# Block moves of an attention kernel: two destination buffers, two issuing queues, fewer tiles moved

## The reference

```python
h = _layernorm(x) * (1 + ca) + sa
x = x + ga * attention(h, w_qkv, w_out)      # 16 heads of 64, causal, softmax over 2048 keys
h = _layernorm(x) * (1 + cb) + sb
x = x + gb * ffn(h, ...)                     # one of 8 experts for each token, 128 -> 512 -> 128, relu
```

## Time and profile before

| | us |
|---|---|
| median of 2 runs (1029.2 to 1029.48) | 1029.34 |
| the profiled execution | 1032.4 |
| its span, first to last instruction | 1030.6 |
| PE busy / VectorE busy / ScalarE busy / GpSimd busy | 919.4 / 758.8 / 626.7 / 110.2 |

### The profile page before, as it was taken

One profiled execution on the slowest core, in us unless ns is written; L12 is line 12 of the kernel. 1 busy time (PEld: TensorE's weight loads), 2 busy tenths in 40 slices (PEclk: granted clock), 3 DMA queues, 4 the chain that ended last, 5 costly groups with the idle time before them and its releaser, 6 DMA issues.

```text
span 1030.6 us, 18821 instructions
## 1 busy us (share of the span) xinstructions
PE 919.4 (89%) x6147; PEld 681.8 (66%) x6147; DVE 758.8 (74%) x2400; ACT 626.7 (61%) x1159; POOL 110.2 (11%) x125
## 2 busy tenths in 40 slices
PE   3999989898998989998989899998999899868797
PEld 2676657675676757675767667675766566546697
DVE  4898748794797848894879578875898389774454
ACT  2876548574685648665757468564875466542375
POOL 0200001000100010000200010001000011101244
PEclk9999989999999999999999999999999899988899
DMA  3005430353014520543036302551053201356020
GB/s 77 11 22 132 106 72 14 90 135 84 21 48 112 120 50 12 127 110 84 14 73 148 87 21 53 127 113 36 23 118 87 66 6 46 95 155 174 25 64 26
DMA packets 154306, 76.91 MB, mean 75 GB/s; under 512 B 20647, under 2 KB 151507, under 8 KB 154210
## 3 DMA queue, kind: packets, MB, share of 16 engines
q1 hardware_dynamic: 152962, 73.58, 29.7%
q0 software_dynamic: 1248, 2.13, 0.7%
HBM read 18.21 MB, written 11.77 MB: 29 GB/s over the span
## 4 chain that ended last, share of the span: by engine, by line
PE 38%; SPq 27%; DVE 17%; DMA 8%; issue 6%; ACT 3%; another core or an unknown queue 1%; POOLq 0%; POOL 0%; DVEq 0%; ACTq 0%
SPq L667 24%; PE ps L910 11%; DMA turned_far<-staged 7%; PE ps L874 6%; PE ps L885 6%; DVE staged L1269 6%; PE ps L853 4%; DVE probs L1254 4%; PE ps L857 3%; PE ps L1034 2%; PE ps L1045 2%; DVE probs L1257 2%; SPq L686 1%; SPq L697 1%; ACT probs L1099 1%
## 5 line engine op out<-in xcount | busy, mean ns | idle before, releaser
L1099 ACT ACTIVATE probs<-probs,neg_max 128x128 f32<-128x128 f32 (+15 forms) x256 | 308.9, 1207 | 150.2 <-DVE neg_max L1261 147.3
L874 PE MATMUL ps<-k_both,q_both 128*128 128x512 f32 (+2 forms) x1280 | 358.8, 397 | 9.0 <-DVE probs L1254 2.8
L1254 DVE TENSOR_SCALAR_CACHE_REDUCE probs<-ps 128x512 f32<-128x512 f32 (+1 forms) x384 | 245.5, 666 | 22.5 <-PE ps L885 10.8
L874 PEld LDWEIGHTS ps<-k_both,q_both 128*128 128x128 f32 x1280 | 203.7, 189 | 78.7 <-issue 28.7
L1107 ACT COPY pT<-ps 128x512 f32<-128x512 f32 (+1 forms) x342 | 178.1, 549 | 113.5 <-PE ps L885 104.8
L885 PE MATMUL ps<-ident,probs 128*128 128x128 f32 x1472 | 213.1, 274 | 1.4 <-ACT probs L1099 0.5
L885 PEld LDWEIGHTS ps<-ident,probs 128*128 128x128 f32 x1472 | 174.8, 141 | 42.3 <-issue 15.4
L910 PE MATMUL ps<-pT,v_sb 128*64 128x256 f32 (+1 forms) x1600 | 174.3, 366 | 9.9 <-DVE oT L1305 7.5
L910 PE MATMUL ps<-turned_far,v_sb 128*64 128x256 f32 x704 | 104.1, 454 | 58.7 <-DMA turned_far<-staged 58.7
L910 PEld LDWEIGHTS ps<-pT,v_sb 128*64 128x64 f32 x1600 | 108.2, 137 | 72.8 <-issue 12.4
L1257 DVE CUSTOM_DVE_ANT_0 probs<-ps,causal 128x256 f32<-128x256 f32 (+3 forms) x256 | 130.6, 510 | 26.4 <-PE ps L874 26.1
(11 more groups left out here) (145 smaller groups left out, 680.5 us busy)
## 6 DMA issues: line engine op xcount, KB each, us to landing
turned_far<-staged SPq DMA_DIRECT2D x384, 96.0 KB
x_sorted<-blank SPq DMA_DIRECT2D x19, 458.5 KB, 5.2
rinv_b<-spread_rows SPq DMA_DIRECT2D x128, 64.0 KB, 2.7
turned_far<-staged SPq DMA_DIRECT2D x128, 64.0 KB
spread_rows<-rinv_rows SPq DMA_DIRECT2D x256, 0.5 KB
probs<-in_L_ffn_W_dram SPq DMA_DIRECT2D x1, 2048.0 KB, 9.5
w_pair<-in_L_attn_w_qkv_dram SPq DMA_DIRECT2D x24, 64.0 KB, 2.1
hT<-x_sorted SPq DMA_DIRECT2D x23, 65.5 KB
```

The source lines that it names most:

```text
L874: m = pe.matmul(ps_ring[:, s.bank, 0:w], q_split[r % 2][:, q0:q0 + P], k_split[r % 2][:, part, k0:k0 + w], start=(part == 0), stop=(part = ...
L1099: act.activation(row, row, ACT.Exp, bias=neg_max[:, g, r:r + 1], accum_out=row_sum[:, g, r:r + 1]).then_inc(exp_done, 1)
L1254: dve.tensor_scalar(row, ps_ring[:, bank, 0:w], 1.0, LOWEST, ALU.mult, ALU.max, accum_out=highest).then_inc(bank_free[bank], 1)
```

## The change

`turned_far` gets two buffers (`FAR_BUFS`), so a move waits for the far value matmuls of the move before the last; `staged` keeps one. SP issues the steps a = 0 and 1 of each move and GpSimd the steps a = 2 and 3, in a list with the K doublings that is sorted by the planner's times. Each destination buffer and each queue has a semaphore of its own, and PE and VectorE wait for both queues' halves. Groups 5, 6 and 7 have 5 far tiles instead of 6, so that 53 of a pair's 72 tiles are near. `pT` has 5 slots instead of 8, and the planner's constants change. The small tables of the last stage lie in `staged` instead of `pT`.

```diff
-PT_SLOTS = 8
-STAGED = 6
-FAR = {4: 4, 5: 6, 6: 6, 7: 6}
-ISSUE = 430.0
+PT_SLOTS = 5
+STAGED = 5
+FAR = {4: 4, 5: 5, 6: 5, 7: 5}
+FAR_BUFS = 2
+ISSUE = 650.0
 LAND = 4000.0
-PV_BATCH = 8
+PV_BATCH = 4
 SCORE_LEAD = 1.4
-SCORE_TILES = 18.0
-TAKE_ACT = 0.0
-TAKE_DVE = 2500.0
-ADD_DVE = 0.0
-PROJ_LEAD = 2
+SCORE_TILES = 16.0
+TAKE_ACT = -800.0
+TAKE_DVE = 600.0
+ADD_DVE = 1000.0
+PROJ_LEAD = 2.5
...
+        steps = [(self.at("lo", p, c, 1), "double", (p, c)) for p, c in parts]
+        for m, (p, g) in enumerate(self.moves):
+            steps += [(self.move_at(m)[0] + 4 * ISSUE * i, "move", (p, g, 2 + i)) for i in range(2)]
+        self.pool = [Step(kind, key, 0, 0) for _, kind, key in sorted(steps)]
...
             begin = max(self.at("shuffle", p, g, r) for r in range(4))
+            if m >= FAR_BUFS:
+                q, f = self.moves[m - FAR_BUFS]
+                begin = max(begin, self.at("pv", q, f, far(f) - 1))
             if m:
-                q, f = self.moves[m - 1]
-                begin = max(begin, self.at("pv", q, f, far(f) - 1), self.move_at(m - 1)[0] + 16 * ISSUE)
+                begin = max(begin, self.move_at(m - 1)[0] + 8 * ISSUE)
...
-            self.moved[m] = begin + HOP, begin + HOP + 16 * ISSUE + LAND
+            self.moved[m] = begin + HOP, begin + HOP + 8 * ISSUE + LAND
...
-            for a in range(4):
+            for a in range(2):
                 steps.append((self.move_at(m)[0] + 4 * ISSUE * a, "move", (p, g, a)))
...
-        turned_far = sb("turned_far", [P, STAGED, P // SQUARE, 4 * SQUARE])
+        turned_far = sb("turned_far", [P, FAR_BUFS, STAGED, P // SQUARE, 4 * SQUARE])
...
+        def move_blocks(queue, key, landed):
+
+            p, g, a = key
+            m = plan.move_no[p, g]
+            queue.wait_ge(shuffled, 4 * m + 4)
+            if m >= FAR_BUFS:
+                q, f = plan.moves[m - FAR_BUFS]
+                queue.wait_ge(pv_done, plan.order[q, f, far(f) - 1] + 1)
+            for b in range(P // SQUARE):
+                queue.dma_start(turned_far[b * SQUARE:(b + 1) * SQUARE, m % FAR_BUFS, 0:far(g), a, :],
+                                staged[a * SQUARE:(a + 1) * SQUARE, 0:far(g), b, :]).then_inc(landed[m % 2], 16)
...
-            for p in range(PAIRS):
-                for c in range(NC):
+            for s in plan.pool:
+                if s.kind == "move":
+                    move_blocks(pool, s.key, moved_soft)
+                    continue
...
-                            pe.wait_ge(moved, 256 * plan.move_no[p, g] + 256)
+                            for landed in (moved, moved_soft):
+                                pe.wait_ge(landed[plan.move_no[p, g] % 2], 128 * (plan.move_no[p, g] // 2) + 128)
...
                     if m and r == 0:
-                        dve.wait_ge(moved, 256 * m)
+                        for landed in (moved, moved_soft):
+                            dve.wait_ge(landed[(m - 1) % 2], 128 * ((m - 1) // 2) + 128)
```

More of the change, by code:

```diff
@@ L508, in adaln_block @@
         blank = sb("blank", [P, ROW])
-        turned_all = pT[:].rearrange("p s c -> p (s c)")
-        hidT = turned_all[:, 0:4 * FF].rearrange("p (s f n) -> p s f n", s=4, f=FT)
-        table_end = [4 * FF]
+        hidT = pT[:, 0:4, :].rearrange("p s (f n) -> p s f n", f=FT)
+        staged_all = staged[:].rearrange("p j b c -> p (j b c)")
+        table_end = [0]
         def table(n, width):
@@ L517, in table @@
             table_end[0] = first + n * width
-            return turned_all[:, first:first + n * width].rearrange("p (r c) -> p r c", c=width)
+            return staged_all[:, first:first + n * width].rearrange("p (r c) -> p r c", c=width)
         PAD_E = NE // 2
@@ L585, in adaln_block @@
         shuffled = sem("shuffled")
-        moved = sem("moved")
+        moved = [sem(f"moved{i}") for i in range(2)]
+        moved_soft = [sem(f"moved_soft{i}") for i in range(2)]
         pv_done = sem("pv_done")
@@ L658, in _ @@
                 if s.kind == "move":
[L659 to L668, removed]
+                    move_blocks(sp, s.key, moved)
                 elif s.kind == "w1":
@@ L716, in _ @@
                                  blank[:].unsqueeze(1).broadcast_to([P, end - first, ROW])).then_inc(blanked, 16)
-            sp.wait_ge(moved, 256 * len(plan.moves))
+            for i in range(2):
+                sp.wait_ge(moved[i], 128 * len(range(i, len(plan.moves), 2)))
+                sp.wait_ge(moved_soft[i], 128 * len(range(i, len(plan.moves), 2)))
             sp.wait_ge(chosen_known, 1)
@@ L763, in _ @@
             pool.wait_ge(numbered, 1)
-            for p in range(PAIRS):
-                for c in range(NC):
[L767 to L779, removed]
+            for s in plan.pool:
+                if s.kind == "move":
+                    move_blocks(pool, s.key, moved_soft)
+                    continue
+                p, c = s.key
+                k_bank, k_use = plan.bank_of("proj", p, c, 1)
+                pool.wait_ge(bank_free[k_bank], k_use + 1)
+                cols = slice(c * BANK, (c + 1) * BANK)
+                for h in range(2):
+                    if h:
+                        pool.wait_ge(k_doubled[c], 2 * p + 1)
+                    elif c:
+                        pool.wait_ge(k_doubled[c - 1], 2 * p + 2)
+                    elif p:
+                        pool.wait_ge(k_doubled[NC - 1], 2 * p)
+                    nc.gpsimd.tensor_copy(k_split[h][own_half(1 - h), :, cols],
+                                          k_split[h][own_half(h), :, cols]).then_inc(k_doubled[c], 1)
             pool.wait_ge(k_doubled[NC - 1], 2 * PAIRS)
@@ L902, in _ @@
                         if j == 0:
-                            pe.wait_ge(moved, 256 * plan.move_no[p, g] + 256)
-                        of_head = turned_far[:, j, :, :].rearrange("p a (u h i) -> p h u a i", u=2, h=2)
+                            for landed in (moved, moved_soft):
+                                pe.wait_ge(landed[plan.move_no[p, g] % 2], 128 * (plan.move_no[p, g] // 2) + 128)
+                        of_head = turned_far[:, plan.move_no[p, g] % FAR_BUFS, j, :, :].rearrange("p a (u h i) -> p h u a i", u=2, h=2)
                     else:
```

## The result

The changed kernel takes 999.72 us (median of 2 runs, 999.27 to 1000.17) where the kernel before takes 1029.34: a ratio of 0.9712, 95% interval 0.9671 to 0.9754. It is faster by 2.9%, and the forecast was 995. The sum came out nearly right, its terms did not: the moves brought much more than I gave them, and the rest of the change took much more back.

What follows compares the result with a forecast made beforehand. TensorE (PE), busy 919.4 of 1030.6 us, bounds the kernel, with 58.7 us of waits for moved blocks. The terms -30 -14 -6 -7 +10 +7 +5 make -35, 997 on the profiled execution, so 995 us; range 977 to 1028.

Steps and rivals of the forecast that it cites:

- The length of a move: Shuffle's end to blocks landed, 15.9 us to use before: SP's half 6.2 us, GpSimd's half landing after 11.9.
- T: GpSimd's time per plain transfer of a move, unknown beforehand: taken as 1.26 us, range 1.0 to 1.55.
- Rival A: GpSimd issues transfers slowly, 1.9 us each, giving 1068 us; chance 0.13 with anything worse than no change, plus 0.04.
- rival C: GpSimd is as quick as SP's path, 1.0 us a transfer; small waits go too, near 983 us; chance 0.13.
- Pair ends: PE's seven waits for group 7's far tiles where a pair ends vanish: -30 us.
- Inside a pair: PE's small waits for moved blocks within pairs: 12 of 17.6 us remain, at group 4, so -6 us.
- The clock: Far matmuls behind the seven pair-end stalls no longer run at the slow clock: -14 us.
- The last pair: Half of PE's 11.1 us wait beside W2's load, and its slow clock, goes: -7 us (0 to -12).
- The tiles: PE turns 24 tiles more because fewer are moved: +10 us.
- Batches: 48 more runs of value matmuls on PE at 0.14 us each: +7 us.
- Weights and reckoned move: Other planner numbers "only reorder" PE's work; together with fewer slots +5 us (0 to 30).
- rival B: The new slots and batches cost 30 us instead of 5, plus 7 of batches: 1020 us; chance 0.20.

Runs made afterwards that it cites:

- e1: Kernel before with only each group's transfers split between SP and GpSimd, planner's reckoning of a move and order kept: 949.61 us, ratio 0.9216.
- e2: Changed kernel, same order and two buffers, but SP issues all 16 transfers of a group: 1158.26 us, ratio 1.1248.
- e5: e1 with 5 far tiles instead of 6 in groups 5, 6 and 7: 967.29 us, ratio 0.9376.
- e6: e1 with runs of value matmuls begun from 4 waiting tiles instead of 8, still 8 slots: 991.28 us, ratio 0.9606.
- e7: e1 with runs of value matmuls from 4 waiting tiles and 5 slots of pT instead of 8: 991.61 us, ratio 0.9601.
- e9: e1 with only the planner's reckoned length of a move changed, 9.3 us from start to landing instead of 10.9: 1002.82 us, ratio 0.9728.
- e11: Changed kernel with 8 slots, runs from 8 tiles and one destination buffer, as before: 989.52 us, ratio 0.9610.
- e3: Changed kernel with one destination buffer on the chip, planner still reckoning with two, same order: 999.31 us, ratio 0.9696.

## Why the prediction was right or wrong

*What bounds it*: right. PE's waits on `turned_far` were the thing to win, and e1 shows it by changing nothing else of the order.

*The length of a move*: wrong in its number. T was 0.573 us, not 1.26, below the range of 1.0 to 1.55 that I kept, and below even SP's 0.611, which I had called the lower bound. I took the nearest row, an indirect DMA; it fetches its rows' places from a table and is another instruction. Rival A (1.9) is refuted, rival C was nearer. The rows that I held against A's mechanism did not bear on it: I put GpSimd's DMAs of the last stage beside VectorE's copies, but they take turns (copies at 999.93 and 1001.83, DMAs at 1000.58 and 1002.48) and never overlap. The half that lands last is SP's, 8.5 us after the shuffle to its last issue, where I had 6.2 for it. The landing of one transfer takes longer than it did with SP alone, in e2 (first row; then the changed kernel; KB each, median us from issue to landing):

```profile
turned_far<-staged SPq DMA_DIRECT2D x384, 80.0 KB, 2.1
```

```profile
turned_far<-staged SPq DMA_DIRECT2D x192, 80.0 KB, 4.3
turned_far<-staged POOLq DMA_DIRECT2D x192, 80.0 KB, 4.0
```

The sum had no term for that, only the old 1.8 us behind the last issue. It cost next to nothing here: PE comes later still, but for the one wait of 0.9 us.

*Pair ends*: right in mechanism, no wait remains. *Inside a pair*: wrong. I left 12 of 17.6 us; 0.9 remain in all, since a move is shorter than the planner reckons, not longer. *The clock*: undersized. I took 14 us from the far matmuls of seven pair ends; e1's busy PE time in the seven pairs fell by 25 with the same instructions. Of the small waits inside the pairs, one had been followed by slow matmuls, 3.58 us for 16 where the others of group 4 take at most 1.95:

```profile
314.30 3.58 PE L910 MATMUL ps<-turned_far,v_sb 128*64 128x256 f32 x16 [2.19 <-DMA turned_far<-staged]
```

The rest of the difference isn't divided. *The last pair*: 7 forecast, 14 in e1. Together these terms say -57 and e1 measured -80.

*The tiles*: +10 forecast; the seven pairs grew by 9 from e1 to e5 for 21 tiles, as forecast, but the whole by 18: most of the rest is in the last pair, whose span goes from 97.5 to 106.5 and holds one wait of 6.1 us on a copy to `pT`. *Batches*: their number was too low (61 for 48), and the price of a run is no constant: 0.11 us of value matmuls in the changed kernel, near my 0.14, but 0.34 in e6, and the whole loss of e6 is 1.2 us a run. *Fewer slots*: nothing in e7, with runs from 4 tiles.

*Weights and reckoned move*: this is the step that failed worst. I wrote that the other planner numbers "only reorder" and put +5 on them and the slots together. On the path above they cost 22, and one of them alone costs 53 (e9). The terms +22 should have been +50: rival B's size, and only a small part of it by B's mechanism, waits on copies to `pT`. The changed kernel has them (PE, then its weight loads, which overlap PE's matmuls):

```profile
PE ps L926 <- ACT pT L1123: 3.8, 8, 0.5
```

```profile
PEld ps L926 <- ACT pT L1123: 15.4, 30, 0.8
```

Before, these were 2.4 and 3.3 us, and in e11, with 8 slots and runs from 8 tiles, 0.2 and 9.7. So at PE itself they make some 4 of the 9.8 us between e11 and e3. So -57 + 22 = -35 was forecast, -80 + 50 = -30 measured. Two errors of about 25 us cancel; that 995 came so near is luck.

*GpSimd's queue*: no visible delay at pair ends; the doubling of the next pair's first K chunk stands at 550.65, seven us before the move of group 7 and behind that of group 6. Until 770 us PE waits 1.5 us on it.

What stays open: which orders are good, and why. e9 shows that the written order alone is worth 53 us, but I haven't traced which of its decisions costs what, and no second good order was found, so whether the one of before is the best with fast moves isn't known.

## What to carry to other kernels

When an engine waits for many small transfers, see whether their landing or their issuing takes the time; where it is the issuing, a second queue shortens it, here from 14.1 to 8.5 us at a pair end, though each transfer then takes longer to land. Where the order of work is written by a planner, run the mechanism first with the order held as it was: here that alone gives 949.6 us, and every kernel with two queues that let the planner write anew was between 963 and 1009. A forecast should never book "it only reorders" at nearly nothing. Look at the last stretch by itself, too: in this kernel a new order often left one wait of 6 to 12 us there.

## What the runs showed of the hardware

A plain DMA issued by GpSimd costs its queue 0.57 us (0.565 to 0.573 in e1 and the changed kernel), its indirect DMAs here 0.96 to 0.98, and SP's 0.61 to 0.63. In their issuing both halves at once slow each other little: SP's median goes from 611 to 627 ns in e1. But a transfer takes twice as long to land: 2.1 us with SP alone (median, 80 KB, e2), 4.3 and 4.0 in the changed kernel. In e1 and the changed kernel VectorE is busy for 80 and 76% of the span, and no plain transfer took GpSimd over 0.81 us to issue. The blocks that go by GpSimd's queue are counted in far fewer packets. Before and in e1, which moves the same bytes:

```profile
q1 hardware_dynamic: 152962, 73.58, 29.7%
q0 software_dynamic: 1248, 2.13, 0.7%
```

```profile
q1 hardware_dynamic: 103810, 50.50, 22.7%
q0 software_dynamic: 12512, 25.21, 11.7%
```

49152 packets and 23.08 MB left the hardware queue, and the same bytes came as 11264 packets on the software queue. And the stalls of this kernel cost half their own length again in PE's busy time: in e1 49 us of idle time went from the seven pairs, and 25 us of busy time with it, some 16 of them by the granted clock.
